# Graph-network and expert-FFN layer on one core: the edge records are transposed by VectorE in 32x32 blocks, and a third PSUM bank takes the tiles' sums

## The reference, cut to what matters

```python
xs, xv = in2f(layernorm(x))               # a table row of 4 x 128 per node
sj, vj = xs[idx_j], xv[idx_j]             # gathered per edge
u = r_ij / norm(r_ij)
h = softplus(f_ij @ Wf1 + bf1) - LOG2
W = (h @ Wf2 + bf2) * rcut_ij[:, None]
m = products of W with sj, vj and u       # 4 groups of 128 are used later
agg = segment_sum(m, idx_i, num_segments=n)
x = x + dense(agg)
x = x + expert_ffn(layernorm(x))          # 8 experts, 312 tokens each
```

## Time and profile before

| | us |
|---|---|
| runs (3), median | 1791.46 |
| lowest, highest | 1783.09, 1799.77 |
| the profiled execution, its own time | 1775.62 |
| its span, first to last instruction | 1773.9 |
| PE busy in the span | 1373.2 (77%) |
| DVE busy | 1077.8 (61%) |
| ACT busy | 839.3 (47%) |
| POOL busy | 746.5 (42%) |

### The profile page before, as it was taken

The page is one execution under the profiler, slowest core; times in us unless marked ns, Lnnn a source line. Parts: engine busy times, 40 slices in busy tenths (PEclk is TensorE's granted clock), DMA queues, the critical chain, the costliest instruction groups (busy, mean ns, idle before and its releaser), DMA issues. The chain is left out here.

```text
span 1773.9 us, 27789 instructions
## 1 busy us (share of the span) xinstructions
PE 1373.2 (77%) x7164; PEld 811.7 (46%) x7164; DVE 1077.8 (61%) x2846; ACT 839.3 (47%) x2239; POOL 746.5 (42%) x798
## 2 busy tenths in 40 slices
PE   0787587777877877787777778777778629999997
PEld 0552344444444444444444444444445525665554
DVE  6899466766676667667676766776677752111110
ACT  3689455555555555555555555555555501111111
POOL 3200455555555555555555555555553011112211
PEclk9989799999999999999999999999999859999999
DMA  5142123333323333333333233332333432645531
GB/s 204 46 170 83 47 76 82 93 87 95 98 82 89 86 94 95 92 99 94 87 109 85 82 82 87 82 82 82 82 82 67 141 115 75 184 141 156 171 77 23
DMA packets 65893, 173.20 MB, mean 98 GB/s; under 512 B 14027, under 2 KB 22619, under 8 KB 65213
## 3 DMA queue, kind: packets, MB, share of 16 engines
q0 software_dynamic: 43648, 106.09, 23.2%
q1 hardware_dynamic: 22196, 66.57, 10.5%
HBM read 149.28 MB, written 18.08 MB: 94 GB/s over the span
## 5 line engine op out<-in xcount | busy, mean ns | idle before, releaser
L1060 PE MATMUL PS<-prod,oneh 128*64 128x256 f32 x2064 | 495.6, 391 | 255.4 <-DVE prod L890 149.8
L540 POOL DMA_INDIRECT gath<-table_d,recs x344 | 325.0, 945 | 406.2 <-PE PS L1060 164.3
L666 ACT ACTIVATE oneh<-oneh,recs 128x64 f32<-128x64 f32 x1032 | 283.5, 338 | 422.4 <-DVE oneh L877 387.3
L1060 PEld LDWEIGHTS PS<-prod,oneh 128*64 128x64 f32 x2064 | 274.6, 140 | 446.6 <-issue 226.7
L901 DVE TENSOR_TENSOR region_s<-region_s,PS 128x512 f32 x344 | 235.2, 684 | 327.9 <-remote 318.7
L529 POOL DMA_INDIRECT recs<-rec_d,inv_i x344 | 324.9, 944 | 209.7 <-issue 181.4
L1053 PE MATMUL PS<-prod,oneh 128*64 128x256 f32 x1376 | 364.8, 400 | 0.0
L1041 PE MATMUL PS<-wf_sb,h_t 128*128 128x512 f32 x688 | 310.5, 594 | 0.0
L673 ACT COPY PS<-c_rep 128x512 f32<-128x512 f32 x340 | 198.9, 585 | 92.2 <-DVE prod L890 89.5
L888 DVE TENSOR_TENSOR prod<-PS,gath 128x384 f32<-128x384 f32 x344 | 187.4, 545 | 0.0
L890 DVE TENSOR_TENSOR prod<-PS,gath 128x384 f32<-128x384 f32 x344 | 187.2, 544 | 0.0
(11 more groups left out here) (272 smaller groups left out, 1537.9 us busy)
## 6 DMA issues: line engine op xcount, KB each, us to landing
region_r<-wu SPq DMA_DIRECT2D x16, 512.0 KB
region_r<-wd SPq DMA_DIRECT2D x16, 512.0 KB
region_u<-wu SPq DMA_DIRECT2D x16, 512.0 KB, 4.3
region_u<-wd SPq DMA_DIRECT2D x16, 512.0 KB, 5.4
recs<-rec_d,inv_i POOLq DMA_INDIRECT x344
gath<-table_d,recs POOLq DMA_INDIRECT x344
region_u<-rec_in SPq DMA_DIRECT2D x1, 5168.0 KB, 17.3
rec_d<-region_u SPq DMA_DIRECT2D x1, 5168.0 KB
```

Source lines behind the costliest of these rows:

```text
L540: nc.gpsimd.indirect_dma_start(out=gath[:, t % GRING, :], out_offset=None, in_=table_d, in_offset=bass.IndirectOffsetOnAxis(ap=recs[:, q % ...
L666: last = nc.scalar.activation(oneh[:, slot, 1 + i, :], oneh[:, slot, 0, :], ACT.Copy, scale=recs[:, r, k, R_VEC + i:R_VEC + i + 1])
L1060: return nc.tensor.matmul(to, oneh[:, slot, 1 + i, :], prod[:, slot, P_Q:P_B + i + 1:1 + i, :], start=i == 0, stop=i == 2, skip_group_chec ...
```

## The change

- `transpose_records` moves from PE to DVE and becomes `nc.vector.transpose`, which transposes each 32 x 32 block of the 128 x 128 piece by itself, SBUF to SBUF. It stands at the end of DVE's step, behind one-hot 3 and ahead of the next quad's products 0, for quad q + 2. The PE transpose, ACT's copy and their semaphore `t_done` go.
- Blocks stay where they are: in `rec_t` row 32k + c, column 32g + e now holds feature c of the edge 32g + e of tile k. PE's `first_layer` reads whole `rec_t` as before, each of its four matmuls now gives tile k's block columns a stride: it writes `ps_h` as `[:, :, k, :]` of `(k g e)`, with 32 adjacent columns and a stride of 128.
- Bank 7 becomes free in the loop. The sums go to banks (0, 1, 7) in turn, so `sum_tile` waits for the flush three tiles back, not two.
- `step` on DVE gets `left` in place of `ahead`, so that the last two quads transpose nothing.

```diff
-SRING = 2
+SRING = 3
+SUM_BANKS = (0, 1, 7)
...
-        ps_t = PS[:, 7, 0:P]
...
-                    scaled_one_hots(t, nxt, 0, 0)
-                    if left >= 2:
-                        evacuate_records(q + 2, (r + 2) % RING)
-                    for k in range(1, QUAD):
+                    for k in range(QUAD):
                         scaled_one_hots(t + k, nxt, k, k)
...
+                def transpose_records(r, body):
+
+                    dve.wait_ge(recs_in[r], 16 * QUAD * body + 16 * QUAD)
+                    nc.vector.transpose(rec_t[:, r, :], recs[:, r].rearrange("p k c -> p (k c)")).then_inc(rec_t_ready, 1)
+
...
                     for k in range(QUAD):
-                        flush(t + k, k % SRING, first=isinstance(q, int) and q == k == 0)
+                        flush(t + k, SUM_BANKS[(QUAD * r + k) % SRING], first=isinstance(q, int) and q == k == 0)
                         if ahead:
                             one_hot(t + QUAD + k, nxt, k, k, nbody)
                         if k == 1 and ahead:
                             hidden(q + 1, nxt)
+                    if left >= 2:
+                        transpose_records((r + 2) % RING, body + (r + 2) // RING)
...
-                def transpose_records(q, r, body):
-                    pe.wait_ge(recs_in[r], 16 * QUAD * body + 16 * QUAD)
-                    hold(pe, rec_t_ready, q + 1, pe_passed)
-                    nc.tensor.transpose(ps_t, recs[:, r].rearrange("p k c -> p (k c)"), ident[:, :]).then_inc(t_done, 1)
-
                 def first_layer(q, r):
 
-                    pe.wait_ge(rec_t_ready, q + 2)
+                    pe.wait_ge(rec_t_ready, q + 1)
                     for k in range(QUAD):
-                        last = nc.tensor.matmul(ps_h[:, k * P:(k + 1) * P], wf1_sb[:, k, :], rec_t[:, r, :],
+                        to = ps_h.rearrange("p (k g e) -> p k g e", k=QUAD, g=QUAD)[:, :, k, :]
+                        last = nc.tensor.matmul(to, wf1_sb[:, k, :], rec_t[:, r, :],
                                                 start=k == 0, stop=k == QUAD - 1, skip_group_check=True)
...
-                        sum_tile(QUAD * q + k, k, k % SRING, first=isinstance(q, int) and q == 0 and k < SRING)
-                        if k == 1 and left >= 2:
-                            transpose_records(q + 2, (r + 2) % RING, body + (r + 2) // RING)
-
-                transpose_records(0, 0, 0)
+                        sum_tile(QUAD * q + k, k, SUM_BANKS[(QUAD * r + k) % SRING],
+                                 first=isinstance(q, int) and q == 0 and k < SRING)
+
```

More of the change, by code:

```diff
@@ L284, in build @@
         rows_in = [sem(f"rows_in{g}") for g in range(GRING)]
-        t_done = sem("t_done")
         rec_t_ready = sem("rec_t_ready")
@@ L641, in _ @@
                 act.wait_ge(s_folded, 4)
[L642 to L646, removed]
                 def size_of_z(q):
@@ L686, in step @@
                     seed(t + 3, 3)
-                    scaled_one_hots(t, nxt, 0, 0)
-                    if left >= 2:
-                        evacuate_records(q + 2, (r + 2) % RING)
-                    for k in range(1, QUAD):
+                    for k in range(QUAD):
                         scaled_one_hots(t + k, nxt, k, k)
-                evacuate_records(0, 0)
                 size_of_z(0)
@@ L696, in _ @@
                 log_of_z(0, first=True)
-                evacuate_records(1, 1)
                 for k in range(QUAD):
@@ L901, in flush, with step @@
                     nc.vector.tensor_tensor(block, block, PS[:, bank, :], ALU.add).then_inc(flushed, 1)
-                def step(q, r, body, ahead=True):
-                    nxt, nbody = (r + 1) % RING, body + (r + 1) // RING
+                def step(q, r, body, left=2):
+                    nxt, nbody, ahead = (r + 1) % RING, body + (r + 1) // RING, left >= 1
                     t = QUAD * q
@@ L914, in step @@
                             hidden(q + 1, nxt)
+                    if left >= 2:
+                        transpose_records((r + 2) % RING, body + (r + 2) // RING)
                 for k in range(QUAD):
                     one_hot(k, 0, k, k, 0, first=True)
+                transpose_records(0, 0)
                 hidden(0, 0)
+                transpose_records(1, 0)
                 for r in range(RING):
@@ L924, in _ @@
                 for q in range(BODIES * RING, QUADS):
-                    step(q, q % RING, q // RING, ahead=q < QUADS - 1)
+                    step(q, q % RING, q // RING, left=QUADS - 1 - q)
             @block.tensor
@@ L1076, in step @@
                     for k in range(QUAD):
-                        sum_tile(QUAD * q + k, k, k % SRING, first=isinstance(q, int) and q == 0 and k < SRING)
-                        if k == 1 and left >= 2:
-                            transpose_records(q + 2, (r + 2) % RING, body + (r + 2) // RING)
-                transpose_records(0, 0, 0)
+                        sum_tile(QUAD * q + k, k, SUM_BANKS[(QUAD * r + k) % SRING],
+                                 first=isinstance(q, int) and q == 0 and k < SRING)
                 first_layer(0, 0)
-                transpose_records(1, 1, 0)
                 for r in range(RING):
```

## The result

The changed kernel takes 2088.43 us in the median (2081.67 to 2103.27, 4 runs), the kernel before beside it 1790.82 (1783.09 to 1799.77, 4 runs): a ratio of 1.167, 95% interval 1.158 to 1.176. Forecast were 1714 us, with a range up to 1890. The profiled execution has a span of 2080.0 us, 306 more than before.

What follows compares the result with a forecast made beforehand. No engine was full; a chain through POOL's gathers and late PE signals (the hold) bound each 13.25 us quad. Saving 0.75 us in 82 quads gave 1775.6 - 62 = 1714 us; own range 1670 to 1750, overall 1630 to 1890.

Steps and rivals of the forecast that it cites:

- The chain: Edge loop: POOL's six gathers, the hold's rest, flush 3, products 0, sum 0, next gather; 13.25 us a quad.
- the hold: PE's signals due some 4 us into POOL's gather run arrive some 1.4 us after its end; flush 3 waits 3.95 us.
- (a): PE loses one transpose a quad, 0.33 us, and ACT one copy, 0.24 us; worth 0.
- (c): DVE gains one transpose a quad, taken as 0.25 us, ahead of products 0; its wait for records costs nothing.
- (b): Third sum bank: PE reaches both layers 1.35 us earlier, and sum 3's signals should slip through before the hold.
- 11.9 and 13.1: Forecast times in us of two alternating quads: sum 3's signal passes in the first and is held in the second.
- the 62 us of gain: Edge loop: mean quad 12.5 us, 0.75 less than 13.25, over 82 quads.
- Rival 2: Flush 3 stays held as now and only the transpose enters: 82 x 0.25 = 20 us, 1796 us; chance 0.13.
- Rival 1: Hold moves to tile 0's `w_ready`, behind eight gathers: quad 14.5 us, 1.2 more, 1874 us; chance 0.38.
- Rival 3: No signal of weight is held any more; POOL's eight gathers bound a quad, 1534 us; chance 0.08.
- (d): PE's first layer writes its output with a stride; no change taken, 0.145 us a pass, at most twice that.

Runs made afterwards that it cites:

- e8: Kernel before with record gathers for the first three quads alone, reused by all later quads; 1535.2 us on a chip where the kernel before takes 1792.
- e14: Kernel before with three small memsets breaking POOL's run of six gathers, once a quad; 1765.52 us, 1.5% faster than before, on a chip with the hold.
- e13: Changed kernel with the transpose moved to the middle of DVE's step and two sum banks; 1796.68 us beside 1792.10, ratio 1.003, with the hold.
- e3: Changed kernel with two sum banks, transpose left at the end of DVE's step; 1643.26 us, 1.061 of the kernel before, without the hold.
- e2: Changed kernel with the transpose in the middle of DVE's step and two sum banks; 1529.78 us, 0.988 of the kernel before, without the hold.
- e5: The changed kernel, unmodified, run again beside the kernel before on a chip with the hold; 2094.78 us, ratio 1.172.
- e7: Changed kernel with the transpose in the middle of DVE's step, three banks; 1867.08 us, 1.043 of the kernel before, with the hold.
- e1: Changed kernel with the transpose in the middle of DVE's step, three banks; 1484.04 us, 0.957 of the kernel before, without the hold.

## Why the prediction was wrong

**The chain, right.** Flush 3 is held, and the hold goes with POOL's run: e8 and e14 show both.

**(a), right where it is held.** PE's transpose and ACT's copy were worth nothing there: mid-step with two banks is 1.003 of before. Without the hold, where the chain is another, the same exchange gains 1.2%.

**(c), the duration right, its place wrong.** 0.25 us was taken; the operation takes 303 ns, and the next on DVE starts 0.22 later (e13: 799.88, 800.10). The 311 ns of the Trainium skill, "VectorE: DVE Perf Modes", "The three transpose paths", given for bf16, are near that. Its wait for records cost nothing, as said. The step that failed is the next: "Behind it stand products 0, and PE's sum 0 waits for those." I named what is queued behind the transpose on DVE and left out who waits for its result. That is PE's first layer of the next quad, at the very start of PE's step; its wait read `q + 2` before and `q + 1` now, which stands in the diff (the number differs only because ACT used to count one signal ahead of the loop). Before, it had been met a step earlier by PE itself and ACT. On DVE the transpose is issued behind one-hot 3, so behind flush 3, the one instruction that is held. The missing term is the way from flush 3 over transpose and layers to products 0, 4.60 - 0.83 = 3.8 us in the quad shown and 5.01 - 0.83 = 4.2 in the one ahead of it, where the sum held 0.25. Taken with what follows from it, the mean quad grew by 3.7 to 3.8 us, 302 to 308 us in 82 quads, and the kernel's profiled execution lost 306. That it is this place and nothing else of the transpose is shown by e3 against e2 (113.5 us, not held) and by e5 against e7 (228 us, held). The other 75 us are the third bank's.

**(b), right in PE, and right on the hold only in some quads.** The gap ahead of the sums is gone (26.4 us to 0.7, and 1.8 in e7). The rest can be judged by e7, where the transpose is out of the way. "Sum 3's signals should slip through before the hold" came true in 15 of its 82 quads, by flush 3's wait of under 0.5 us; in 10 more flush 3 was let go after 1.1 to 1.8 us, with POOL still issuing. In the quad of 817.35 it did not: PE begins the first layer at 812.15, 3.56 us after the run's start at 808.59 (before: 808.45 - 803.64 = 4.81), and flush 3 is held all the same. So a start of the hold at 4 us, read from one pair of signals, is no limit. Where flush 3 went early, the forecast's next step, that `w_ready` 0 passes in mid-run, mostly failed: in 16 of the 25 quads products 0 start 1.9 to 2.0 us behind POOL's eighth gather. In a few they did start while POOL was still issuing (760.13, 933.51), but the two quads around 755.55 take 9.36 and 17.82, not 11.9 and 13.1. With that the 62 us of gain fell, and the third bank costs where signals are held.

**The rivals.** Rival 2's "flush 3 still waits 3.9 us" is what the trace of the changed kernel shows (3.8), but its price, only the 0.25 us, lacked the same term. Rival 1's mechanism, the hold that moves to `w_ready` 0 behind eight gathers, is seen in e7, with its lower clock and 1.3 us more for sum 0; it isn't what lost the changed kernel its 228 us. Its sum has a wrong sign: the 0.2 in front of PE is to be added, 814.75 + 1.26 + 0.21 + 2.29 = 818.5, a cycle of 14.9 us and about 1909 us for the kernel, not 1874. The layers' slower clock behind the hold nobody had. Rival 3 isn't seen on held chips; e1 shows it on another: nothing waits for "remote", POOL issues its gathers with hardly a break, and a quad takes 10.2 us in the mean, with PE at 98% (294.60 us of the 300 from 700 on).

**(d)** was right: the first layer's row is 1.16 us for eight in e7 and e13 too, as in the earlier trace rows.

## What to carry to other kernels

When an operation changes engines, list who waits for its result and where that waiter stands in its own engine's order, and then ask what the operation is queued behind on the new engine. Here the same 0.3 us transpose was free in the middle of DVE's step and cost 7% at its end (two banks), 12% where the instruction ahead of it was held (three banks). One more buffer is a gain only if no later wait takes it back: the third bank gained 3% on some chips and cost 4% on others.

## What the runs showed of the hardware

- The same program takes 1791 us on some chips and 1549 on others, in three jobs and in four. In the traces of the first kind some of PE's signals arrive only when POOL's run of indirect gathers has ended, and DVE, POOL and ACT wait for "remote". In the twelve traces of the second kind no engine has such a wait between 300 and 1300 us. A gather takes 943 to 948 ns in both. Why this is so isn't known from any run here.
- A run of gathers alone doesn't make the hold: in e1, on a chip of the second kind, POOL issues them 1.25 us apart with hardly a break.
- Before the change flush 3 starts 1.4 to 1.6 us behind the run's end in 75 of 82 quads. In the changed kernel this holds in 26 of 84 (POOL's gather of 923.18 ends at 924.12 and flush 3 starts at 925.64), and in 24 it starts only 0.1 to 0.2 behind it (942.19, 942.30).
- Where the hold is, three memsets of 0.35 us a quad in POOL's queue made the kernel 1.5% faster, and leaving out half the gathers 14%.
- After 5 to 7 us in which PE had nothing to do, eight passes of the first layer took 2.08 us in place of 1.16, with a granted clock of 0.76 and 0.86 over the two quads around it.

```profile
907.00:926.50 19.50, 12.26 (x56) 7.36 (x56) 10.00 (x25) 7.43 (x19) 7.75 (x9) 0.76 0.22 59
925.60:944.60 19.00, 12.38 (x61) 8.09 (x62) 10.58 (x25) 8.36 (x22) 8.89 (x10) 0.86 0.22 59
```

The clock stands third from the right; in a plain quad before it was 1.00.

- What the changed kernel would take on a chip without the hold wasn't run. From 1643 and the bank's 46 it would be about 1597 us, an estimate that assumes that the two add up. Two banks with the transpose at the step's end weren't run on a held one.
